# Feed-forward stage of a graph network: outputs kept in two PSUM banks, the layer norm per block on ScalarE, its scale and shift folded into the weights

## Chip, cores and metric

One NeuronCore of a Trainium2 chip runs the whole program in one launch. The metric is device time in microseconds (us); lower is better. The kernel before takes 7056.64 us (median of 3 runs, 7054.48 to 7057.89).

## What is computed

Six attention layers over a graph of 3,125 nodes (128 features each) and 100,000 edges, with normalised residual blocks around them. The change touches one stage alone, the one that stands between the first attention layer (8 heads, "gat") and the second ("tconv"). Of the reference, cut to that stage:

```python
h = elu(gat(x, ...)); h = x + h                      # x here: relu(layernorm(stream))
mu = mean(h); var = var(h)
ln = (h - mu) * rsqrt(var + 1e-05) * ln_gamma + ln_beta
inter = relu(ln @ W1 + b1)                            # 128 -> 512
stream = stream + inter @ W2 + b2 + h                 # 512 -> 128
x = relu(layernorm(stream))                           # input of the next layer
q, k, v, skip = x @ Wq + bq, x @ Wk + bk, x @ Wv + bv, x @ Wskip + bskip
```

`ln_gamma`, `ln_beta` and `b1` are not trivial here (drawn at random).

## The kernel before, in words

The program is a row of stages, each a block with its own instruction stream per engine and a barrier at its end: one that sets up the graph, and then by turns `node_stage` (work on the nodes) and `edge_sweep` (work on the edges; it gathers node rows from tables in HBM and writes partial sums to `part_tab`). The sweeps take most of the time. The changed stage is the second `node_stage`, called with `after="ffn"`.

The 25 blocks of 128 nodes (partition = node, free = feature) are worked in four chunks: blocks 0 to 3, then three chunks of 7. `chunks` holds these. Nothing is scheduled by a planner: the order on every engine is the order of the calls in the program, and engines meet at semaphores.

The stage begins by joining the sweep's partial sums (`tiles()`); then GpSimd gathers the 25 blocks' sums (`own`, L1319). Per chunk `c` there are then these pieces:

- **VectorE, `join(c)` and `use(c)`**: divide by the softmax sums (L1581 to L1585), elu with the exponential taken on ScalarE (L1636 to L1639; `elus(c)`, L1462), the moments of each row (`mean_and_spread`: L1598, L1601; the square root on ScalarE is `roots(c)`, L1457; L1606, L1607), the normalised rows into `hn` (L1642, one instruction per block), and times gamma (L1644) and plus beta (L1645) over the chunk.
- **TensorE, `feed_forward(c)`**: per block a transpose (`ffn_turn`, L1393), the product with W1 into a PSUM bank (`ffn_hidden`, L1399, 4 matmuls of 128 columns, which the profile records as 8) and the product with W2 (`ffn_out`, L1407, the same number). ScalarE stands between them: `ffn_copy` (L1467) moves the transposed block to SBUF, `ffn_relu` (L1473, 4 instructions) adds b1, clips and moves the hidden rows.
- **VectorE, `feed_forward(c)`**: the stream plus h (L1650), and plus each block's output (L1653) as it comes out of one of two banks `ffn_ps`; then `mean_and_spread` of the stream, which lets ScalarE's `inputs(c)` go.
- **The projections**: ScalarE's `inputs(c)` normalises the stream (L1492) and copies its transpose (L1507); TensorE's `multiply(c)` transposes (L1378) and multiplies (L1388, 512 columns) into one of two banks; VectorE's `products(c)` adds the bias and writes three tiles per block (L1664). SyncE stores `kv_tab` per chunk (L1291), GpSimd scatters the block's q rows to `q_tab` (L1329).

ScalarE and VectorE run these by steps, and this is what sets the order around the change. ScalarE's loop:

```python
for step in range(len(chunks) + 2):
    if step < len(chunks):
        elus(step); roots(step)
    if 1 <= step <= len(chunks):
        feed_forward(step - 1); roots(step - 1)
    if step >= 2:
        inputs(step - 2)
```

VectorE does `join(step)`, `use(step)`, `feed_forward(step - 1)`, `mean_and_spread(step - 1)` and `products(step - 2)` in each step, TensorE `feed_forward(step - 1)` and `multiply(step - 2)`.

## Time and profile before

| | us |
|---|---|
| median of 3 runs | 7056.64 |
| the profiled execution, its own time | 7060.29 |
| its span in the profile | 7058.2 |
| the stage's chunks, first `own` rows used to last product written | 1372.36 to 1510.13 |
| first instruction of the next sweep's VectorE | 1519.53 |

| engine | busy us of the span | in 1372 to 1519.5 |
|---|---|---|
| TensorE | 4367.5 | 91.36 |
| VectorE | 5261.5 | 80.79 |
| ScalarE | 3157.8 | 63.99 |
| GpSimd | 4812.4 | 45.92 |

Times in the trace count from the span's start. A row of the timeline gives an instruction or a run of like instructions with its start, its length and, in square brackets, how long its engine had been idle before it and what ended that. PE is TensorE's matmul, PEld its weight load, DVE VectorE, ACT ScalarE, POOL GpSimd. The granted clock (PEclk) is a share of TensorE's full 2.4 GHz; 0.50 is the lower level, 1.2 GHz.

### The profile page before, as it was taken

Reading aid. Unit: us, or ns where it says so; the run is one execution under the profiler, and the core shown is the slowest. Engines: PE = TensorE matmul, PEld = TensorE weight load, DVE = VectorE, ACT = ScalarE, POOL = GpSimd, SP = SyncE. Lnnn points to the kernel's source line nnn. Section 1 sums busy time; section 2 is a strip of 40 time slices with the busy share of each in tenths; the row PEclk is TensorE's granted clock in tenths of the full one; section 3 lists DMA queues with packets and bytes.
Section 4 is the critical chain, followed back from the end, with each engine's and each line's share of the span. In section 5 each row is a group of like instructions: output and inputs, shape, how many; then the busy total and the mean of one; then the engine's idle time right before and its main releaser. Section 6 shows DMA issues by size and latency. Waiting matters only on the chain. (4 is left out here: it accounts for less than half of the span.)

```text
span 7058.2 us, 100657 instructions
## 1 busy us (share of the span) xinstructions
PE 4367.5 (62%) x25901; PEld 3913.4 (55%) x25901; DVE 5261.5 (75%) x9430; ACT 3157.8 (45%) x5509; POOL 4812.4 (68%) x5080
## 2 busy tenths in 40 slices
PE   2665656467777747777755666654666664666663
PEld 1555656456666636666644555553555553555553
DVE  5766667658888848888865666655888885888887
ACT  1666666444444414444423444433555552555552
POOL 4766666347777757777757777766777774777774
PEclk6666666688898868888877777776777776777876
DMA  2777777449999949999956888864666663666663
GB/s 73 197 196 195 197 201 205 122 136 296 299 292 298 294 125 294 299 296 297 293 166 207 244 244 244 243 201 121 198 197 197 198 199 89 197 197 198 199 197 105
DMA packets 1275821, 1491.03 MB, mean 211 GB/s; under 512 B 395524, under 2 KB 967587, under 8 KB 1275252
## 3 DMA queue, kind: packets, MB, share of 16 engines
q1 hardware_dynamic: 1075428, 991.23, 44.8%
q0 software_dynamic: 199824, 493.36, 25.2%
q8 instruction: 217, 3.56, 0.2%
q14 instruction: 352, 2.88, 0.1%
HBM read 1065.64 MB, written 418.20 MB: 210 GB/s over the span
## 5 line engine op out<-in xcount | busy, mean ns | idle before, releaser
L760 POOL DMA_INDIRECT s_rows<-kv_tab,src_col x2346 | 2218.7, 946 | 733.9 <-issue 688.3
L905 PE MATMUL bank<-s_msg,s_hot 128*128 128x144 f32 (+1 forms) x9408 | 1770.3, 344 | 299.5 <-ACT s_part L800 280.9
L760 POOL DMA_INDIRECT s_rows<-xl_tab,src_col x1564 | 1476.3, 944 | 489.4 <-issue 443.5
L880 PE MATMUL bank<-s_qwin,s_hot_t 128*128 128x128 f32 (+1 forms) x9408 | 1608.7, 326 | 289.8 <-DVE s_prod L1020 156.1
L905 PEld LDWEIGHTS bank<-s_msg,s_hot 128*128 128x128 f32 x9408 | 1565.5, 239 | 352.6 <-ACT s_part L800 308.4
L880 PEld LDWEIGHTS bank<-s_qwin,s_hot_t 128*128 128x128 f32 x9408 | 1513.2, 245 | 312.0 <-issue 182.8
L800 ACT ACTIVATE s_part<-bank 128x288 f32<-128x288 f32 (+1 forms) x2352 | 914.6, 402 | 809.2 <-PE bank L905 762.8
L783 ACT ACTIVATE s_gap<-s_ranks,minus_id 128x1024 bf16<-128x1024 bf16 x588 | 673.1, 1145 | 982.4 <-DMA s_ranks<-rank_tab 980.5
L760 POOL DMA_INDIRECT s_rows<-gat_tab,src_col x782 | 739.8, 946 | 390.4 <-issue 236.3
L895 PE MATMUL bank<-ident,s_alpha 128*32 128x128 f32 (+1 forms) x588 | 185.2, 315 | 1002.3 <-DVE s_msg L1057 850.9
L794 ACT ACTIVATE s_prob<-s_diff 32x128 f32<-32x128 f32 (+1 forms) x588 | 180.5, 307 | 1233.1 <-DVE s_diff L969 1184.2
L953 DVE TENSOR_TENSOR s_hot<-bank,rank_col 128x1024 f32<-128x1024 f32 x588 | 714.7, 1215 | 0.0
L1053 DVE TENSOR_TENSOR s_msg<-s_rows,bank 128x1024 f32<-128x1024 f32 x588 | 711.6, 1210 | 0.0
L1022 DVE TENSOR_REDUCE s_alpha<-s_prod 128x16 f32<-128x512 f32 (+1 forms) x980 | 672.4, 686 | 33.6
L1020 DVE TENSOR_TENSOR s_prod<-bank,s_rows 128x512 f32<-128x512 f32 x588 | 405.6, 690 | 384.7 <-DMA s_rows<-kv_tab,src_col 357.4
L787 ACT ACTIVATE s_hot_t<-s_gap,one 128x1024 f32<-128x1024 bf16 x588 | 675.1, 1148 | 19.3
L1011 DVE TENSOR_TENSOR s_rows<-s_rows,bank 128x1024 f32<-128x1024 f32 x392 | 475.6, 1213 | 271.4 <-DMA s_rows<-kv_tab,src_col 237.6
L895 PEld LDWEIGHTS bank<-ident,s_alpha 128*32 128x32 f32 (+1 forms) x588 | 65.4, 111 | 1101.9 <-issue 1101.4
L877 PE MATMUL bank<-We,s_attr_t 128*128 128x128 f32 x3136 | 512.2, 315 | 201.7 <-DVE s_prod L1020 137.1
L877 PEld LDWEIGHTS bank<-We,s_attr_t 128*128 128x128 f32 x3136 | 445.9, 219 | 231.7 <-issue 155.5
L997 DVE TENSOR_TENSOR bank<-bank,s_rows 128x512 f32<-128x512 f32 x392 | 253.9, 692 | 166.1 <-DMA s_rows<-xl_tab,src_col 138.3
L919 PE MATMUL bank<-ident,s_attr 128*128 128x128 f32 x784 | 173.4, 363 | 300.3 <-ACT s_attr L819 291.5
(301 smaller groups left out, 4771.3 us busy)
## 6 DMA issues: line engine op xcount, KB each, us to landing
s_qwin<-q_tab SPq DMA_DIRECT2D x3920, 64.0 KB
part_tab<-s_part SPq DMA_DIRECT2D x294, 576.0 KB
part_tab<-s_part SPq DMA_DIRECT2D x294, 544.0 KB
s_ranks<-rank_tab SPq DMA_DIRECT2D x588, 256.0 KB
s_attr_t<-attr_tab SPq DMA_DIRECT2D x196, 512.0 KB
attr_tab<-s_attr_t SPq DMA_DIRECT2D x98, 512.0 KB, 5.5
s_rows<-kv_tab,src_col POOLq DMA_INDIRECT x2346
s_rows<-xl_tab,src_col POOLq DMA_INDIRECT x1564
```

The source lines that it names most:

```text
L760: pool.indirect_dma_start(out=rows[u][:, t, :], out_offset=None, in_=tab, in_offset=bass.IndirectOffsetOnAxis(ap=pl.src_col[:, i * G + t:i ...
L783: act.activation(gap[:, :], ranks[u][:, :], ACT.Abs, bias=pl.minus_id[:, 0:1]).then_inc(gap_done, 1)
L787: act.activation(hot_t[u % 2][:, :], gap[:, :], ACT.Relu, scale=-1.0, bias=pl.one[:, 0:1]).then_inc(hot_t_built, 1)
L800: act.activation(part[u][:, PAIR * c:PAIR * (c + 1), :], part_ps[c % 2][:, 0:PAIR * W].rearrange("p (t w) -> p t w", t=PAIR), ACT.Copy).th ...
L877: pe.matmul(e_ps[h][:, (t - h * per) * D:(t - h * per + 1) * D], attr_t[u][:, t * P:(t + 1) * P], w["We"][:, :], start=True, stop=True)
L880: ins = pe.matmul(q_ps[h][:, (t - h * per) * QW:(t - h * per + 1) * QW], hot_t[u % 2][:, t * P:(t + 1) * P], qwin[u][:, t, :], start=True, ...
L905: ins = pe.matmul(part_ps[c % 2][:, t * W:(t + 1) * W], hot[u][:, PAIR * c + t, :], msg[u % 2][:, PAIR * c + t, :], start=True, stop=True)
L953: v.tensor_tensor(hot[u][:, :, :], bc(iota_ps.unsqueeze(1), [P, G, P]), bc(pl.rank_col[:, bass.ds(i * G, G)].unsqueeze(2), [P, G, P]), ALU ...
L1011: v.tensor_tensor(kv, kv, bc(e.unsqueeze(2), [P, HALF, 2, D]), ALU.add).then_inc(e_used, 1)
L1020: v.tensor_tensor(prod[h][:, :, :], q, rows[u][:, t0:t1, 0:D], ALU.mult).then_inc(q_used, 1)
L1022: v.tensor_reduce(alpha[:, t0:t1, :], prod[h][:, :, :].rearrange("p t (h c) -> p t h c", c=C), AX.X, ALU.add).then_inc(alpha_done, 1)
L1053: v.tensor_tensor(out[:, :, 0:D].rearrange("p t (h c) -> p t h c", c=C), vals.rearrange("p t (h c) -> p t h c", c=C), bc(p.unsqueeze(3), [ ...
```

## The change

- A chunk's feed-forward outputs (up to 7 blocks of 128 columns) all stay in the two banks `ffn_ps`, four blocks to a bank. VectorE adds them with two instructions once the whole chunk is there. TensorE waits, ahead of a chunk's first output, until the chunk before was added.
- The normalised rows are made by ScalarE, a block at a time (`ffn_norm`), up to three blocks ahead of the block that is multiplied. Times gamma and plus beta are gone: `w1` is multiplied by gamma once, row by row, and `b1_col` gets W1ᵀ·beta, from four matmuls of one column ahead of the first chunk. Two row loads become two column loads.
- ScalarE does `feed_forward(c)` before it turns to chunk `c + 1`: `elus(c + 1)` stands behind the second block of chunk `c`, `roots(c + 1)` behind the fourth. The square roots of the stream, `roots(c - 1)`, come after chunk `c`'s first three norms; `inputs(c - 1)` follow `feed_forward(c)`.
- VectorE takes `products(c - 1)` inside `mean_and_spread(c)` of the stream, between the moments and the wait for the roots.

```diff
+            gamma_col, beta_col = sb("gamma_col", [P, 1]), sb("beta_col", [P, 1])
...
-        rows = [sb(f"row{n}", [P, D]) for n in range(len(vectors))]
+        row_vectors = vectors[2:] if after == "ffn" else vectors
+        rows = [sb(f"row{n}", [P, D]) for n in range(len(row_vectors))]
...
+                    for t, a in ((gamma_col, vectors[0]), (beta_col, vectors[1])):
+                        sp.dma_start(t[:, :], a.rearrange("(p a) -> p a", a=1), allow_slow_non_contiguous=True
+                                     ).then_inc(ffn_loaded, 16)
...
+                if after == "ffn":
+                    pe.wait_ge(ffn_loaded, 16 * 5)
+                    for k in range(PARTS):
+                        ins = pe.matmul(ps[1][:, k:k + 1], w1[:, k * P:(k + 1) * P], beta_col[:, :], start=True, stop=True)
+                    ins.then_inc(b1_folded, 1)
...
                 def ffn_turn(b):
+                    pe.wait_ge(ffn_normed, b + 1)
...
-                def ffn_out(b):
+                def ffn_out(b, slot):
                     pe.wait_ge(hidden_used, b + 1)
-                    wait(pe, ffn_added, b - 1)
+                    to = ffn_ps[slot // 4][:, (slot % 4) * D:(slot % 4 + 1) * D]
                     for k in range(PARTS):
-                        ins = pe.matmul(ffn_ps[b % 2][:, 0:D], hidden[b % 2][:, k, :], w2[:, k, :], start=(k == 0),
-                                        stop=(k == PARTS - 1))
+                        ins = pe.matmul(to, hidden[b % 2][:, k, :], w2[:, k, :], start=(k == 0), stop=(k == PARTS - 1))
                     ins.then_inc(ffn_done, 1)
...
                 def feed_forward(c):
                     if c == 0:
-                        pe.wait_ge(ffn_loaded, 48)
+                        pe.wait_ge(ffn_weights, 1)
                     lo, hi = chunks[c]
-                    pe.wait_ge(ffn_ready, c + 1)
                     ffn_turn(lo)
                     for b in range(lo, hi):
                         if b + 1 < hi:
                             ffn_turn(b + 1)
                         ffn_hidden(b)
                         if b > lo:
-                            ffn_out(b - 1)
-                    ffn_out(hi - 1)
+                            wait(pe, ffn_added, c)
+                            ffn_out(b - 1, b - 1 - lo)
+                    wait(pe, ffn_added, c)
+                    ffn_out(hi - 1, hi - 1 - lo)
...
+                def ffn_norm(b):
+                    act.activation(pl.hn[:, b, :], h[:, b, :], ACT.Identity, scale=rstd[:, b:b + 1], bias=shift[:, b:b + 1]
+                                   ).then_inc(ffn_normed, 1)
+
                 def feed_forward(c):
+                    act.wait_ge(ffn_ready, c + 1)
+                    lo, hi = chunks[c]
+                    for b in range(lo, lo + 3):
+                        ffn_norm(b)
                     if c == 0:
-                        act.wait_ge(ffn_loaded, 48)
-                    lo, hi = chunks[c]
+                        act.wait_ge(ffn_weights, 1)
+                    else:
+                        roots(c - 1)
                     ffn_copy(lo)
                     for b in range(lo, hi):
+                        if b + 3 < hi:
+                            ffn_norm(b + 3)
                         if b + 1 < hi:
                             ffn_copy(b + 1)
                         ffn_relu(b)
+                        if c + 1 < len(chunks) and b == lo + 1:
+                            elus(c + 1)
+                        if c + 1 < len(chunks) and b == lo + 3:
+                            roots(c + 1)
...
-                    for step in range(len(chunks) + 2):
-                        if step < len(chunks):
-                            elus(step)
-                            roots(step)
-                        if 1 <= step <= len(chunks):
-                            feed_forward(step - 1)
-                            roots(step - 1)
-                        if step >= 2:
-                            inputs(step - 2)
+                    elus(0)
+                    roots(0)
+                    for c in range(len(chunks)):
+                        feed_forward(c)
+                        if c >= 1:
+                            inputs(c - 1)
+                    roots(len(chunks) - 1)
+                    inputs(len(chunks) - 1)
...
-                    if proj and c >= 1 and after != "ffn":
+                    if proj and c >= 1 and x is not pl.res:
...
-                    link(mean_and_spread(c, h))
-                    for b in range(lo, hi):
-                        ins = v.tensor_scalar(pl.hn[:, b, :], h[:, b, :], rstd[:, b:b + 1], shift[:, b:b + 1], ALU.mult, ALU.add)
-                    link(ins)
-                    link(v.tensor_tensor(pl.hn[:, s, :], pl.hn[:, s, :], bc(rows[0][:, :].unsqueeze(1), [P, n, D]), ALU.mult))
-                    return v.tensor_tensor(pl.hn[:, s, :], pl.hn[:, s, :], bc(rows[1][:, :].unsqueeze(1), [P, n, D]), ALU.add)
+                    return mean_and_spread(c, h)
...
                 def feed_forward(c):
                     lo, hi = chunks[c]
                     link(v.tensor_tensor(pl.x_sb[:, lo:hi, :], pl.x_sb[:, lo:hi, :], h[:, lo:hi, :], ALU.add))
-                    for b in range(lo, hi):
-                        v.wait_ge(ffn_done, b + 1)
-                        v.tensor_tensor(pl.x_sb[:, b, :], pl.x_sb[:, b, :], ffn_ps[b % 2][:, 0:D], ALU.add).then_inc(ffn_added, 1)
-                    v.wait_ge(ffn_added, hi)
+                    v.wait_ge(ffn_done, hi)
+                    for n, b in enumerate(range(lo, hi, 4)):
+                        e = min(b + 4, hi)
+                        ins = v.tensor_tensor(pl.x_sb[:, b:e, :], pl.x_sb[:, b:e, :],
+                                              ffn_ps[n][:, 0:(e - b) * D].rearrange("p (b d) -> p b d", d=D), ALU.add)
+                    ins.then_inc(ffn_added, 1)
+                    v.wait_ge(ffn_added, c + 1)
...
+                    v.wait_ge(b1_folded, 1)
+                    link(v.tensor_tensor(b1_col[:, :], b1_col[:, :], ps[1][:, 0:PARTS], ALU.add))
+                    v.tensor_scalar(w1[:, :], w1[:, :], gamma_col[:, 0:1], None, ALU.mult).then_inc(ffn_weights, 1)
+                    for step in range(len(chunks) + 1):
                         if step < len(chunks):
                             join(step)
                             use(step).then_inc(ffn_ready, 1)
-                        if 1 <= step <= len(chunks):
+                        if step >= 1:
                             feed_forward(step - 1)
                             mean_and_spread(step - 1, pl.x_sb).then_inc(input_ready, 1)
-                        if step >= 2:
-                            products(step - 2)
+                    products(len(chunks) - 1)
```

ScalarE around the start of chunk 1's feed-forward, before (`s_below` holds the arguments and results of elu's exponential, `s_std` the roots, `s_ffn_t` the transposed block, `s_hidden` the hidden rows; L1457 128x4 is the stream of chunk 0, L1457 128x7 h of chunk 2):

```order
L1473 ACTIVATE s_hidden<-bank,s_b_col 128x128 x8
L1457 ACTIVATE s_std<-s_moments,eps 128x4
L1462 ACT_TABLE_LOAD
L1462 ACTIVATE s_below<-s_below 128x896
L1457 ACT_TABLE_LOAD
L1457 ACTIVATE s_std<-s_moments,eps 128x7
L1467 ACTIVATE s_ffn_t<-bank 128x128 x2
L1473 ACTIVATE s_hidden<-bank,s_b_col 128x128 x4
L1467 ACTIVATE s_ffn_t<-bank 128x128
L1473 ACTIVATE s_hidden<-bank,s_b_col 128x128 x4
```

The same place in the change, from the roots of chunk 1's h on (L1491 is the norm, L1480 the copy, L1486 the relu, L1475 the exponential):

```order
L1470 ACTIVATE s_std<-s_moments,eps 128x7
L1491 ACTIVATE hn<-res,s_shift,s_rstd 128x128 x3
L1470 ACTIVATE s_std<-s_moments,eps 128x4
L1480 ACTIVATE s_ffn_t<-bank 128x128
L1491 ACTIVATE hn<-res,s_shift,s_rstd 128x128
L1480 ACTIVATE s_ffn_t<-bank 128x128
L1486 ACTIVATE s_hidden<-bank,s_b_col 128x128 x4
L1491 ACTIVATE hn<-res,s_shift,s_rstd 128x128
L1480 ACTIVATE s_ffn_t<-bank 128x128
L1486 ACTIVATE s_hidden<-bank,s_b_col 128x128 x4
L1475 ACT_TABLE_LOAD
L1475 ACTIVATE s_below<-s_below 128x896
```

The exponential of chunk 2 and its table load have moved from before chunk 1's first copy to behind its second relu.

VectorE in the third step, before, from the last piece of chunk 2's `use` on (`s_q_rows` is the first write of `products(0)`, of which two more for each block follow):

```order
L1642 TENSOR_SCALAR hn<-res,s_rstd,s_shift 128x128 x7
L1644 TENSOR_TENSOR hn<-hn,s_row 128x896
L1645 TENSOR_TENSOR hn<-hn,s_row 128x896
L1650 TENSOR_TENSOR x_sb<-x_sb,res 128x896
L1653 TENSOR_TENSOR x_sb<-x_sb,bank 128x128 x7
L1598 BN_STATS s_stats<-x_sb 128x6 x7
L1601 BN_AGGR s_moments<-s_stats 128x2 x7
L1606 RECIPROCAL s_rstd<-s_std 128x7
L1607 SCALAR_TENSOR_TENSOR s_shift<-s_moments,s_rstd 128x7
L1664 TENSOR_TENSOR s_q_rows<-bank,s_bias 128x128
```

The same place in the change:

```order
L1672 TENSOR_TENSOR x_sb<-x_sb,res 128x896
L1676 TENSOR_TENSOR x_sb<-x_sb,bank 128x512
L1676 TENSOR_TENSOR x_sb<-x_sb,bank 128x384
L1625 BN_STATS s_stats<-x_sb 128x6 x7
L1628 BN_AGGR s_moments<-s_stats 128x2 x7
L1689 TENSOR_TENSOR s_q_rows<-bank,s_bias 128x128
```

The norm, gamma and beta are gone, seven adds are two, and the products of chunk 0 stand ahead of L1606 and L1607 (now L1633 and L1634), no longer behind them.

## Rows read from the trace of the kernel before

**Rows 1.** Busy time by stretch: stretch, length, PE, PEld, DVE, ACT, POOL, PEclk, DMA, GB/s.

```profile
1388.87:1399.34 10.47, 10.13 (x68) 9.92 (x68) 5.71 (x15) 5.13 (x19) 8.33 (x8) 0.77 0.24 58
...
1409.25:1425.46 16.21, 15.86 (x117) 15.48 (x117) 7.00 (x18) 9.08 (x34) 0.00 (x0) 0.85 0.00 1
1425.46:1444.30 18.84, 7.46 (x14) 3.11 (x14) 12.85 (x51) 6.86 (x15) 3.92 (x4) 0.74 0.11 42
1444.30:1460.07 15.77, 15.43 (x117) 15.04 (x117) 6.99 (x18) 8.97 (x34) 0.00 (x0) 0.88 0.01 2
1460.07:1474.09 14.02, 10.54 (x23) 4.33 (x23) 8.04 (x37) 5.13 (x17) 4.84 (x5) 0.76 0.05 19
1474.09:1488.52 14.43, 13.85 (x117) 13.28 (x117) 3.14 (x9) 8.97 (x34) 1.94 (x2) 1.00 0.22 78
1488.52:1510.13 21.61, 17.21 (x42) 6.67 (x42) 14.16 (x59) 9.29 (x29) 10.72 (x12) 0.92 0.20 74
```

**Rows 2.** Waits of TensorE from 1372 to 1519: total us, times, longest.

```profile
PE bank L1399 <- ACT s_ffn_t L1467: 25.7, 4, 9.7
PE bank L1393 <- DVE hn L1645: 23.2, 1, 23.2
PE bank L1378 <- ACT hn L1492: 9.6, 3, 3.2
```

**Rows 3.** Timeline, chunk 0 up to its first hidden product.

```profile
1372.36 0.18 DVE L1581 TENSOR_SCALAR s_share<-s_own 128x32 f32<-128x32 f32 x1 [6.32 <-DMA s_own<-part_tab,part_i]
...
1377.69 0.16 DVE L1607 SCALAR_TENSOR_TENSOR s_shift<-s_moments,s_rstd 128x4 f32<-128x4 f32 x1
...
1379.77 0.69 DVE L1645 TENSOR_TENSOR hn<-hn,s_row 128x512 f32<-128x512 f32 x1
...
1381.26 0.21 DVE L1581 TENSOR_SCALAR s_share<-s_own 128x56 f32<-128x56 f32 x1 [0.81 <-DMA s_own<-part_tab,part_i]
```

**Rows 4.** Timeline, chunk 2's join and elu ahead of chunk 1's feed-forward.

```profile
1401.65 0.20 DVE L1581 TENSOR_SCALAR s_share<-s_own 128x56 f32<-128x56 f32 x1
...
1404.46 0.95 ACT L1462 ACTIVATE s_below<-s_below 128x896 f32<-128x896 f32 x1 [1.84 <-DVE s_below L1636]
1405.43 1.28 ACT L1457 ACT_TABLE_LOAD   x1
...
1408.74 0.30 ACT L1457 ACTIVATE s_std<-s_moments,eps 128x7 f32<-128x7 f32 x1 [2.03 <-DVE s_moments L1601]
```

**Rows 5.** Timeline, one round of the block loop at full clock.

```profile
1417.53 1.15 ACT L1473 ACTIVATE s_hidden<-bank,s_b_col 128x128 f32<-128x128 f32 x4 [0.58 <-PE bank L1399]
...
1418.22 0.97 PEld L1399 LDWEIGHTS bank<-s_ffn_t,s_w 128*128 128x128 f32 x8
...
1418.54 0.29 ACT L1467 ACTIVATE s_ffn_t<-bank 128x128 f32<-128x128 f32 x1
...
1420.12 0.97 PEld L1399 LDWEIGHTS bank<-s_ffn_t,s_w 128*128 128x128 f32 x8
```

**Rows 6.** Timeline, two ScalarE norms of 128x128 with scale and shift from tiles.

```profile
1499.58 0.87 ACT L1492 ACTIVATE hn<-x_sb,s_shift,s_rstd 128x128 f32<-128x128 f32 x2
```

**Rows 7.** The page's costliest groups: a VectorE operation of 128x512 that reads PSUM.

```profile
L1020 DVE TENSOR_TENSOR s_prod<-bank,s_rows 128x512 f32<-128x512 f32 x588 | 405.6, 690 | 384.7 <-DMA s_rows<-kv_tab,src_col 357.4
```

**Rows 8.** Timeline, the moments of the stream after chunk 1.

```profile
1425.82 1.45 DVE L1598 BATCH_NORM_STATS2 s_stats<-x_sb 128x6 f32<-128x128 f32 x7
1427.31 0.58 DVE L1601 BATCH_NORM_AGGREGATE s_moments<-s_stats 128x2 f32<-128x6 f32 x7
```

**Rows 9.** Timeline, the stage's end and the next sweep's first instruction.

```profile
1512.63 0.97 POOL L1329 DMA_INDIRECT q_tab<-s_q_rows,compact_i  x1 [0.30 <-issue]
1519.53 0.29 DVE L1086 COPY bank<-iota_free 128x128 f32<-128x128 f32 x1 [9.41 <-PEq L1242]
```

**Rows 10.** Timeline, TensorE in a later sweep after two equal idle times.

```profile
1702.18 0.27 PE L895 MATMUL bank<-ident,s_alpha 128*32 128x128 f32 x1 [2.45 <-DVE s_msg L1057]
...
1711.09 0.37 PE L895 MATMUL bank<-ident,s_alpha 128*32 128x128 f32 x1 [2.45 <-DVE s_msg L1057]
```

More of the change, by code:

```diff
@@ L1191, in node_stage @@
             hidden_ps, ffn_ps = ps[4:6], ps[6:8]
-            ffn_loaded = sem("ffn_loaded")
+            assert most <= 8
+            gamma_col, beta_col = sb("gamma_col", [P, 1]), sb("beta_col", [P, 1])
+            ffn_loaded, b1_folded, ffn_weights = sem("ffn_loaded"), sem("b1_folded"), sem("ffn_weights")
+            ffn_normed = sem("ffn_normed")
             elu_args, elu_exps, ffn_ready = sem("elu_args"), sem("elu_exps"), sem("ffn_ready")
@@ L1245, in _ @@
             def _(sp):
-                for t, a in zip(rows, vectors):
+                for t, a in zip(rows, row_vectors):
                     sp.dma_start(t[:, :], a.partition_broadcast(P)).then_inc(vectors_loaded, 16)
@@ L1618, in use @@
                         if c == 0:
-                            v.wait_ge(vectors_loaded, 16 * len(vectors))
+                            v.wait_ge(vectors_loaded, 16 * len(rows))
                         r = [bc(t[:, :].unsqueeze(1), [P, n, D]) for t in rows]
@@ L1686, in _ @@
                 if after == "norm_stream":
-                    v.wait_ge(vectors_loaded, 16 * len(vectors))
+                    v.wait_ge(vectors_loaded, 16 * len(rows))
                     link(v.tensor_tensor(pl.x_sb[:, :, :], pl.x_sb[:, :, :], bc(rows[2][:, :].unsqueeze(1), [P, NB, D]), ALU.add))
@@ L1693, in _ @@
                 if after == "ffn":
-                    v.wait_ge(vectors_loaded, 16 * len(vectors))
-                    link(v.tensor_tensor(pl.x_sb[:, :, :], pl.x_sb[:, :, :], bc(rows[2][:, :].unsqueeze(1), [P, NB, D]), ALU.add))
-                    for step in range(len(chunks) + 2):
+                    v.wait_ge(vectors_loaded, 16 * len(rows))
+                    link(v.tensor_tensor(pl.x_sb[:, :, :], pl.x_sb[:, :, :], bc(rows[0][:, :].unsqueeze(1), [P, NB, D]), ALU.add))
+                    v.wait_ge(b1_folded, 1)
+                    link(v.tensor_tensor(b1_col[:, :], b1_col[:, :], ps[1][:, 0:PARTS], ALU.add))
+                    v.tensor_scalar(w1[:, :], w1[:, :], gamma_col[:, 0:1], None, ALU.mult).then_inc(ffn_weights, 1)
+                    for step in range(len(chunks) + 1):
                         if step < len(chunks):
```

## Prediction

> **What bounds the stage now.** The sweeps that fill the program are not touched, so only the stretch from 1372.36 to 1519.53 counts, 2% of the span. I cut it where TensorE passes from one chunk's piece to the next and read busy times by stretch [rows 1]. While a chunk's feed-forward runs TensorE is nearly full: 15.86 of 16.21 us, 15.43 of 15.77, 13.85 of 14.43. Between these stretches it is not: 7.46 of 18.84 us, 10.54 of 14.02, and next to nothing from 1399.34 to 1409.25. TensorE's waits name the cause [rows 2]: 25.7 us for ScalarE's copies ahead of W1's product in four chunks, 23.2 us for the first chunk's rows from VectorE, 9.6 us for the stream's norm. The copies are late by order alone. In step 2 ScalarE takes chunk 2's exponential at 1404.46, loads a table, takes the root at 1408.74, and only then turns to chunk 1, whose rows VectorE had finished in the step before [rows 4]. So what bounds the stage is VectorE's chain for the next chunk, put in series with this chunk's matmuls. The clock adds to it: stretches that open after a gap are granted 0.74 to 0.88 on average, the one without a gap before it 1.00 [rows 1].
>
> **The change, step by step.** I write the new order forward from the old durations, each instruction starting when its engine is free and its semaphore in. Every start below is an estimate from those rows.
>
> *Start of chunk 0.* Shift is done at 1377.85; L1642, gamma and beta end at 1380.46, and then the copy waits for chunk 1's exponential and root, so that the first hidden product starts at 1388.87 [rows 1, 3]. Now three norms on ScalarE follow at once. Two such take 0.87 us, 0.39 apart [rows 6], so the third is issued by 1378.8, the copy goes at 1379.3, the product at 1379.6. Gain **9.3**.
>
> *Folding gamma and beta.* Four one-column matmuls on TensorE, an add of four columns and a scaling of 128x512 on VectorE, ahead of chunk 0. The trace has none of these. From below they cost nothing: VectorE is idle for 6.32 us before the first rows land [rows 3]. From above they would be 0.69 us for the 128x512 one [rows 7] and as much again for the rest, still inside that idle time. I take nothing. If the loads were late it would be TensorE's gap before chunk 0, which is now short. Two row loads become two column loads at the same number of issues: nothing.
>
> *Chunk 0 to chunk 1.* Gathered rows of chunk 1 land at 1381.26 [rows 3]; join and clip take 2.8 us to the exponential (1401.65 to 1404.46 [rows 4]), so arguments are there at 1384.1. ScalarE reaches that place behind its second relu at 1385.1, loads a table (1.28), and the exponential (0.95) ends at 1387.4. VectorE's elu and moments take it to 1390.6, ScalarE's table load and root to 1391.5, VectorE's shift to 1392.0. VectorE then adds h, then four blocks of output (0.69 [rows 7]), and takes the stream's moments, to 1394.8; ScalarE's stream root and the copy follow; chunk 1's first hidden product starts at 1395.3. Before, 20.4 us passed between the two first products (1388.87 to 1409.25), now 15.7. Gain **4.6**.
>
> *A chunk's block loop.* At full clock a round is 1.90 us on TensorE (1418.22 to 1420.12). ScalarE's relu takes 1.01 to the next issue, with 0.58 us idle before it, and its copy fits [rows 5]. A norm of 0.39 us [rows 6] fits into the 0.58. It is paid when that cover is gone, at 1.2 GHz never (a round is 3.8 us), at full clock only behind a table load. Those are new in the loop: an exponential with its load (2.23) after the second block and a root with its load (1.6) after the fourth. TensorE has about 1.1 us of work left when ScalarE turns away, and ScalarE then needs a norm and a copy before it can go on, so each costs 1 to 1.5 us. Chunk 1 also opens at full clock if its gap is short. 14.4 us at full clock [rows 1] plus 2.1 gives 16.5 against 16.2 for chunk 1 and against 15.8 for chunk 2: loss **0.3** and **0.7**. Chunk 3 has neither, 14.4 as before: **0**.
>
> A new wait stands in TensorE's queue: output one of a chunk until VectorE has added the chunk before. VectorE does that right behind the next chunk's shift, at least 6 us before TensorE asks in chunks 2 and 3: nothing. From above, its two adds of 1.25 us.
>
> *Chunk 1 to chunk 2.* Before, 18.84 us [rows 1]: stream moments, root, products(0), then all of chunk 3's join and moments. Now ScalarE has the inputs of chunk 0 ready, so TensorE multiplies at once, fills both banks, and waits for VectorE: two adds 1.25, moments 1.45 and 0.58 and their links [rows 8], 3.4 in all. Then four blocks at about 1 us; the copy for chunk 2 waits only for the fourth. 7.0 us. Gain **11.8**. *Chunk 2 to chunk 3.* 14.02 before; now the same 3.4 and seven blocks, 10.4. Gain **3.6**.
>
> *Tail.* 21.61 before, in which products(2) began after moments and root. Now they begin before the root, but products(3) follow only after the root, norm, transpose and copy: a hole of 2.9. 21.3. Gain **0.3**. The next sweep starts 9.4 us after the last product and 6.9 after the last scatter [rows 9]. Scatters are 1.27 apart and end 1.5 us behind the products instead of 2.5, so what ends last gains 0 to 1 more.
>
> Sum: −9.3 −4.6 +0.3 −11.8 +0.7 −3.6 −0.3 = −28.6, and with half of that last point **−29**. The profiled execution is 7060.29, 3.65 above the median. 7056.64 − 29 = 7027.6, say **7028**.
>
> One unknown is the table load inside the loop. Row 1405.43 shows 1.28 us, 0.02 behind the end of the instruction before [rows 4]; I take 1.28. The Trainium skill (ScalarE: Activation LUTs, "What ACT_TABLE_LOAD costs") speaks against this change: it counts a switch of sets as about 2.66 us, with a drain of the engine ahead of the load. By that page six loads would cost an estimated 8 us more.
>
> **Rivals.**
> - *The clock falls in the new small gaps.* My order leaves eight idle times of 1.1 to 2.0 us on TensorE. In a later sweep 2.45 us idle once left the clock high (a 0.27 us matmul) and once did not (0.37) [rows 10], so it can go either way. Were the clock low after each gap, chunks would open slow as now. About 4.8 us at half speed costs 2.4 per chunk and more in the products; written forward that is 13 us: **7041**. For it: chunk 0's stretch is short and broken. Against: the one stretch that opened without a gap was granted 1.00 throughout [rows 1].
> - *The chunk at hand does not come first.* If chunk c+1's arguments come later than ScalarE reaches the exponential, ScalarE stands there and TensorE behind it. My margin is 1.0 us in chunk 0 and 1.4 in chunk 1. With 2 to 3 us lost in each of three chunks: **7036**.
> - *Loads that stop ScalarE for longer.* Inside the loop the engine has relus in flight when a load comes. If each of the six loads there cost as long again as its row (1.28 us [rows 4]), 7.7 us more: **7036**. Against: the load at 1405.43 started 0.02 behind an exponential.
> - *Slower.* The clock stays at 1.2 GHz through the stage because no stretch is unbroken. Then a round is 3.8 and a product 2.1 us, 25 blocks take 147.5 us from 1379.6, and with the tail's latency the last product is at 1529 against 1510.13: 19 us slower, **7076**. It decides once the granted clock of the stage is below about 0.65. Against: stretches of 14 us with TensorE full remain.
> - *Nothing is gained*, because the barrier or the next sweep's first loads wait for something else. Against: 9.4 us of the end are idle on every engine but GpSimd. **7057**.
>
> **Chances.** My forecast 0.66; clock in the gaps 0.13; chunk at hand 0.10; dearer loads 0.05; slower 0.02; nothing 0.04. What is more, my forward writing, laid over the old order, ended 5 us late, mostly in stretches at the lower clock, of which the change has fewer. A measurement of this kernel can tell 0.2%, 14 us, from no change: faster means below 7042.5. My forecast, the chunk-at-hand case and the dearer loads lie there (0.81), and of the clock case somewhat over half: 0.89. Within 0.2%: 0.08. Slower: 0.03. The range goes down to 7018 (the waits behind table loads not paid, the clock high throughout, 9 more) and up to 7042, which takes in the clock rival.
>
> **What would show it.** Right: TensorE's first hidden product about 1380, 9 us earlier; its waits for ScalarE's copies down from 25.7 to below 8 us; the stretch from chunk 1's last output to chunk 2's first hidden product 7 us; the next sweep's first VectorE instruction near 1491; everything behind it shifted whole. Wrong: a granted clock below 0.85 between 1395 and 1481; ScalarE waiting for `s_below` inside a chunk; L1642's work on ScalarE longer than 0.48 us each; rounds above 2 us in chunk 3, where nothing was added but the norm.

## The result, and the profile after

The change takes **7029.32 us** (median of 6 runs, 7026.59 to 7037.12), the kernel before 7057.27 on the same chip (6 runs, 7053.62 to 7066.97): a ratio of 0.996, 95% interval 0.9947 to 0.9973. It is 28 us faster, 0.4%; 7028 was predicted.

The profiled execution took 7037.12 us, its span is 7035.3. The spans differ by 22.9 us only. The first sweep, which the change does not touch, took longer in this execution: the first gathered rows are used at 1380.44, not 1372.36. In six profiles with that sweep unchanged the moment lies anywhere from 1365.1 to 1380.4, so whole spans can't be compared to within 15 us. I count from that moment, called A. From A to the next sweep's first VectorE instruction 147.17 us passed before, 119.12 now: **−28.05**. The rest of the program took 5538.7 and 5535.7.

Eight of the twelve experiments ran in two lots of four, each lot on one chip, on which every kernel took 9,678 to 9,991 us. The kernel before took 9938.13 us beside the first lot (next chunk first, products behind roots, banks by block, order alone) and 9867.58 beside the second (the change again, norm on VectorE, norm with gamma and beta on VectorE, last root early). I read them by stretches of the stage. The change ran in the second lot only, so each difference between the first lot and the change also contains whatever sets the two chips apart.

Busy time by stretch, the change, cut where TensorE passes between the pieces (length, PE, PEld, DVE, ACT, POOL, granted clock, DMA share, GB/s):

```profile
1387.48:1402.71 15.23, 11.44 (x69) 10.43 (x69) 9.85 (x34) 10.87 (x30) 11.88 (x12) 0.83 0.20 50
1402.71:1420.55 17.84, 16.14 (x119) 15.21 (x119) 8.27 (x25) 14.70 (x44) 3.84 (x4) 0.90 0.10 22
1420.55:1427.16 6.61, 4.57 (x15) 1.84 (x13) 5.87 (x27) 3.42 (x12) 1.98 (x2) 1.00 0.03 10
1427.16:1443.90 16.74, 14.71 (x119) 13.65 (x119) 8.70 (x28) 14.57 (x44) 1.94 (x2) 1.00 0.14 45
1443.90:1453.89 9.99, 7.91 (x25) 3.08 (x22) 8.33 (x36) 5.40 (x18) 4.43 (x5) 1.00 0.08 26
1453.89:1468.43 14.54, 13.79 (x119) 13.44 (x119) 1.66 (x5) 11.09 (x40) 3.20 (x3) 1.00 0.24 78
1468.43:1490.19 21.76, 17.25 (x42) 6.42 (x40) 14.73 (x60) 8.62 (x27) 11.71 (x13) 0.92 0.24 77
```

The gain is in four places. Chunk 0's first hidden product comes 9.5 us earlier and chunk 1's another 5.2 (table below). Against [rows 1] two passages are shorter: from chunk 1's last output to chunk 2's first hidden product 6.61 us instead of 18.84, and one chunk later 9.99 instead of 14.02. The blocks of chunks 1 and 2 take longer (17.84 us for 16.21, 16.74 for 15.77), those of chunk 3 and the tail hardly (14.54 for 14.43, 21.76 for 21.61). TensorE's waits in the stage, the change:

```profile
PE bank L1406 <- ACT hn L1491: 20.8, 2, 19.4
PE bank L1412 <- ACT s_ffn_t L1480: 4.9, 6, 1.9
PE bank L1400 <- DVE res L1689: 4.6, 3, 1.5
...
PE bank L1390 <- ACT hn L1520: 1.8, 1, 1.8
```

ScalarE's copies ahead of W1's product held TensorE for 25.7 us before [rows 2], now for 4.9. The long wait of 19.4 reaches back to before A, for the first rows.

| us from A | before | predicted | change |
|---|---|---|---|
| first hidden product, chunk 0 | 16.51 | 7.2 | 7.04 |
| chunk 1 | 36.9 | 22.9 | 22.3 |
| chunk 2 | 71.9 | 46.4 | 46.7 |
| chunk 3 | 101.7 | 73.4 | 73.5 |
| last product written | 137.77 | 109.2 | 109.75 |
| next sweep's first VectorE instruction | 147.17 | 118.2 | 119.12 |

### The profile page after: what moved, and what is told of

It reads as the page before. It is cut to its first block and busy times, and to the rows that moved or that the text cites. A ratio compares the mean times of both kernels' runs of the same rounds, so it can differ in the third digit from the quotient of the medians.

```text
span 7035.3 us, 100670 instructions
## 1 busy us (share of the span) xinstructions
PE 4351.4 (62%) x25909; PEld 3895.3 (55%) x25909; DVE 5245.4 (75%) x9381; ACT 3165.3 (45%) x5534; POOL 4810.8 (68%) x5080
## 5 line engine op out<-in xcount | busy, mean ns | idle before, releaser
L877 PE MATMUL bank<-We,s_attr_t 128*128 128x128 f32 x3136 | 497.2, 308 | 196.1 <-DVE s_prod L1020 133.5
```

Source lines behind the costliest of these rows:

```text
L877: pe.matmul(e_ps[h][:, (t - h * per) * D:(t - h * per + 1) * D], attr_t[u][:, t * P:(t + 1) * P], w["We"][:, :], start=True, stop=True)
```

## Experiments

My theory: the gain comes from ScalarE's order (chunk at hand first), and it can be had only because the two banks hold a chunk's outputs while VectorE is at the next chunk; the norm's place and the folding only shorten the start. The rivals are that one part alone does it, above all the shorter VectorE work (norm, gamma and beta gone), or the banks.

**The next chunk first again.** On ScalarE chunk c + 1's exponential and root stand once more ahead of chunk c's copies; all else is as in the change.

```diff
+                    if c + 1 < len(chunks):
+                        elus(c + 1)
+                        roots(c + 1)
                     ffn_copy(lo)
...
-                        if c + 1 < len(chunks) and b == lo + 1:
-                            elus(c + 1)
-                        if c + 1 < len(chunks) and b == lo + 3:
-                            roots(c + 1)
```

> The change with one part undone: ScalarE takes the next chunk's exponential and root (elus(c + 1), roots(c + 1)) ahead of this chunk's first copy, as before. Read as the stretch from the first gathered rows used to the next sweep's first VectorE instruction: 147.2 us in the kernel before, 119.1 in the change. Theory (the order on ScalarE is the gain): each of chunks 0 to 2 again waits for VectorE's join and moments, 8 to 9 us each, 24 in all: 143 us, and TensorE's waits for ScalarE's copies back above 25 us. Rival (the gain is the smaller work, gamma, beta and norm off VectorE and two adds for seven): 120 to 124 us.

The last product is written at A + 140.24; the change has 123.97 in the second lot (below). Since the start of the stage was not clean there, the kernel ran again later, with the kernel before beside it at 7064.49 us:

> The kernel of e1 (the next chunk's exponential and root ahead of this chunk's feed-forward) on another chip, since chunk 0 was disturbed there. There chunk 1's first hidden product to chunk 2's took 31 us against 24.7 in the change, and what followed was as long. Theory (order on ScalarE): chunk 0 then loses about 9 us before its first product and 6 more before chunk 1's, the stretch is 139 to 143 us, and the whole kernel 7050 us, within 10 of before. Rival (most of the difference was the disturbance): stretch below 130.

7059.22 us (10 runs, 7055.22 to 7065.34) against 7064.49 of before (19 runs): ratio 0.9991, 0.9981 to 1.0. From A to the next sweep 139.71 us: 20.6 more than the change, 7.5 less than before. TensorE's waits:

```profile
PE bank L1412 <- ACT s_ffn_t L1480: 29.8, 4, 10.9
PE bank L1406 <- ACT hn L1491: 19.3, 1, 19.3
```

With ScalarE's old order the copies' wait is back, at 29.8 us for the 25.7 of [rows 2], though the norm, the folding, the banks and VectorE's early products are those of the change. Of what is lost, 10.9 us lie ahead of chunk 0's first product (A + 17.91), 5.0 between it and chunk 1's and 6.1 between chunk 1's and chunk 2's. With all the rest in place, ScalarE's order decides over most of the gain.

**Order alone.** Here norm, gamma and beta are on VectorE as before, and the outputs go out block by block; only the orders of the change are kept (with its wait for the chunk's rows on TensorE).

> The new order alone: banks by block, norm, gamma and beta on VectorE as before; only the order of the calls is the change's. Theory: without the banks and the shorter VectorE chain the new order gives nothing, stretch 147 us as before (138 from first rows to last product). Rival (the order is the gain whatever the rest): 125 to 130 us.

A + 150.03 to the last product, which by itself says little with the start disturbed. Run again beside the last one:

> The kernel of e8 (the new order with banks by block and norm, gamma and beta on VectorE) on another chip. Theory: stretch 147 us, as before the change, and a whole time within 0.1% of before: order alone gives nothing. Rival: a part of the gain remains, stretch 130 to 140.

7062.41 us (7056.61 to 7069.19), ratio 0.9994, 0.9984 to 1.0003: no gain. From A to the next sweep 146.06 us, 1.1 less than before. Chunk 0's first product comes at A + 9.15 instead of 16.51 and chunk 1's at 32.4 instead of 36.9, but from chunk 0's to chunk 1's 23.3 us pass instead of 20.4 and from chunk 2's to chunk 3's 35.0 instead of 29.8, and that takes most of it back. Its waits name why:

```profile
PE bank L1414 <- DVE x_sb L1672: 26.2, 3, 8.9
...
PE bank L1405 <- ACT s_ffn_t L1473: 3.2, 6, 1.8
```

The copies' wait is down to 3.2 us, as in the change, and one as long (26.2) has come in its place: TensorE has filled both banks after two blocks and needs VectorE to empty one, and VectorE is at the next chunk's join, elu, moments and norm. The last of that, ahead of the longest of these waits:

```profile
1420.11 1.89 DVE L1661 TENSOR_SCALAR hn<-res,s_rstd,s_shift 128x128 f32<-128x128 f32 x7
1422.03 1.09 DVE L1663 TENSOR_TENSOR hn<-hn,s_row 128x896 f32<-128x896 f32 x1
1423.16 1.09 DVE L1664 TENSOR_TENSOR hn<-hn,s_row 128x896 f32<-128x896 f32 x1
...
1425.72 0.55 PE L1414 MATMUL bank<-s_w,s_hidden 128*128 128x128 f32 x1 [8.88 <-DVE x_sb L1672]
```

So the order alone is worth 1.1 us, and the change with only ScalarE's part of the order undone 7.5; together they are worth 28.0. The two runs don't split the change into exact halves, for VectorE's early products stand in both, but the sum of 8.6 shows that most of the gain belongs to neither by itself.

**The change again, in the second lot.**

> The change once more, a second profile. The stage from the first gathered rows to the next sweep's first VectorE instruction should be 119.1 us again, within 0.5, if the order of semaphores fixes it. The first sweep, which the change does not touch, took 8 us longer in the change's profile than in that of before: if that is a matter of the execution, it comes out otherwise here; if it is the change's doing, it stays.

9768.71 us for the whole program. The first product of chunk 0 is at A + 7.05, as in the first profile; then about 14 us are lost between A + 15 and A + 33, so the 119.1 us of the expectation became 133.2. From chunk 1's first product on, the steps (to chunk 2's, to chunk 3's, to the last product) are 24.7, 27.3 and 35.7 us, where the first profile of the change has 24.45, 26.7 and 36.3. The two other kernels that ran under both conditions agree less well: next chunk first has 30.7, 25.8 and 37.4 against 30.6, 25.8 and 36.0, order alone 33.0, 37.2 and 36.4 against 34.1, 35.0 and 35.25. So a step can be read in these lots to within about 2 us, the start can't. All that follows up to the last two runs was measured there.

**Banks by block.** The change with one block's output per bank, freed by VectorE's add of that block.

```diff
+                    wait(pe, ffn_added, b - 1)
+                    to = ffn_ps[b % 2][:, 0:D]
...
+                    for b in range(lo, hi):
+                        v.wait_ge(ffn_done, b + 1)
+                        v.tensor_tensor(pl.x_sb[:, b, :], pl.x_sb[:, b, :], ffn_ps[b % 2][:, 0:D], ALU.add).then_inc(ffn_added, 1)
```

> One part undone: outputs go to the two banks by turns, block by block, and VectorE adds each block by itself; the rest as in the change. Theory (the banks are what lets a chunk run while VectorE works on the next): TensorE stops at a chunk's third output until VectorE is through with the next chunk's moments, 4 to 6 us in each of chunks 0 to 2, and the stretch is 135 us. Rival (the banks only save VectorE instructions): 119 to 121 us.

The last product comes at A + 139.63, 15.7 us behind the change's 123.97; 4.0 of it lie in the disturbed start. The steps are 29.4, 33.7 and 36.2 us; the last, where no next chunk is joined, is as in the change, so the rest of the cost lies only where VectorE has a next chunk. The wait is named as with the order alone:

```profile
PE bank L1421 <- DVE x_sb L1674: 18.5, 3, 8.6
```

Order alone, of the same lot, differs from this kernel only in the norm, gamma and beta on VectorE, and its last product comes 10.4 us later (150.03); its first two steps are 3.5 us longer each, its last as long. Without the banks for a whole chunk that work of VectorE stands between TensorE and the bank it waits for.

**Products behind the roots.** VectorE takes the projections' products of chunk c − 1 again behind its mean and spread, and ScalarE takes the stream's root right behind the chunk's feed-forward.

```diff
                         feed_forward(c)
+                        roots(c)
                         if c >= 1:
                             inputs(c - 1)
-                    roots(len(chunks) - 1)
```

> One part undone: VectorE takes products(c - 1) behind the stream's root and shift, and ScalarE takes that root right behind feed_forward(c), ahead of inputs(c - 1), as before (the two go together, since each would wait for the other otherwise). Theory: TensorE again waits out moments, root and join between two chunks, about 5 us at each of three places beside a short tail: stretch 135 us. Rival (the products' place is worth the start of the tail alone): 122 to 123 us.

Last product at A + 142.19, 18.2 us later than the change; the steps are 28.9, 32.5 and 42.9 us, all three longer. In the last one ScalarE stood 3.28 us with no semaphore behind it, so that some 15 of the 18 us are the move's, an estimate. TensorE's wait for the stream's norm, once 1.8 us, is now

```profile
PE bank L1390 <- ACT hn L1518: 12.4, 3, 4.1
```

in each of the three passages. I had given this move little weight in the prediction, where it stands only as "multiplies at once". It is worth about as much as the banks.

**The norm on VectorE, folding kept.** `ffn_norm` is empty and VectorE writes the seven normalised blocks behind the shift.

> One part undone: the norm is made on VectorE (one instruction per block, 1.9 us for seven), gamma and beta stay folded. Theory: it lies on the path only at chunk 0 and 1, where VectorE's chain ends last; ScalarE saves as much: stretch 120 us, first hidden product of chunk 1 some 2.5 us later than in the change. Rival (ScalarE's norms fill its loop and stretch the rounds, so that VectorE would be the better place): 116 to 118 us.

Chunk 0 starts at A + 7.71 (+0.66) and the last product comes at 123.69, 0.3 before the change; chunk 1 starts 1.0 later, not 2.5. With the banks and the folding in place, which engine does the norm makes nothing that I can tell.

**Norm, gamma and beta on VectorE.** As the one before, and gamma and beta are applied to rows as in the kernel before, with no folding.

> The norm, times gamma and plus beta all on VectorE as before, nothing folded; order and banks as in the change. Theory: 4.1 us more of VectorE's chain per chunk, of which only 2 us at chunk 0, 4 at chunk 1 and little later is on the path: stretch 125 us. Rival (VectorE's chain is on the path in every chunk): 119 + 2.6 + 3 x 4.1 = 134 us.

Chunk 0 starts at A + 9.14 (+2.1), the last product comes at 126.24: +2.3. The steps are 24.0, 26.7 and 35.3 us, none longer than the change's, so what it costs lies before chunk 1; the disturbed start of both runs leaves the size open by a few microseconds, the sign and the place are plain. With a chunk's outputs in the banks, VectorE's smaller work is thus a small part of the 28 us; without them it was worth the 10.4 above.

**The last root early.** The change's only hole in the tail: with ScalarE's last root behind the fourth copy of `inputs(2)`, and VectorE's reciprocal and shift behind four of seven blocks of `products(2)`.

> A further step: the last chunk's stream root is taken by ScalarE behind the fourth copy of inputs(2), and VectorE's reciprocal and shift inside products(2), so that chunk 3's projections follow chunk 2's without a hole. Theory (the hole of 2.4 us and the slower clock behind it are on the path): last product 3 to 4 us earlier, but scatters at 1.27 us each then end last, 14 of them: stretch 116 to 117 us. Rival (scatters set the end already): 118.5 to 119 us.

Inconclusive. The last product came at A + 125.75, 1.8 later, and in the tail ScalarE and VectorE stood once each, 3.75 and 3.38 us, with no semaphore behind it, as in the lost 14 us. The last step took 38.85 us; less 3.75 it would be 35.1 against the change's 35.7, an estimate and within what these lots can tell.

**Products ahead of the stream's moments.** This goes further, and was timed beside the change on an undisturbed chip. VectorE takes `products(c - 1)` ahead of the moments of chunk c's stream; in the last chunk two blocks, then the moments, three more, the spread, and the rest. On ScalarE the stream's root comes behind the first relu instead of ahead of the first copy, and the exponential and the root of the next chunk one block later each in chunks 1 and 2 (in chunk 0 they stay). The last root comes behind the fifth copy of `inputs(2)`.

```diff
-                    else:
-                        roots(c - 1)
                     ffn_copy(lo)
...
+                        if c >= 1 and b == lo:
+                            roots(c - 1)
-                        if c + 1 < len(chunks) and b == lo + 1:
+                        if c + 1 < len(chunks) and b == lo + min(c + 1, 2):
                             elus(c + 1)
-                        if c + 1 < len(chunks) and b == lo + 3:
+                        if c + 1 < len(chunks) and b == lo + min(c + 3, 4):
                             roots(c + 1)
...
+                    if after == "ffn" and x is not pl.res and c >= 1:
+                        products(c - 1, last=chunks[c - 1][0] + 2 if c == len(chunks) - 1 else None)
                     for b in range(lo, hi):
                         ins = v.bn_stats(stats[:, b, :], x[:, b, :])
```

> A version meant to beat both. Beside the early last root of e6, VectorE does products(c - 1) ahead of the stream's moments of chunk c (in the last chunk two blocks ahead of them), so that TensorE's banks come free 2.1 us sooner between two chunks; ScalarE takes the stream's root behind the first relu, and the next chunk's exponential and root one block later. Written forward from the same durations: each of three passages 1.5 to 2.5 us shorter, the stretch from first gathered rows to the next sweep 111 to 112 us where the change takes 119.1 on an undisturbed chip. Rival (the exponential's arguments then come too late and ScalarE stands): no shorter than the change. The whole kernel would be 7 us below the change, a tenth of a per cent, less than its times can tell: 0.995 of before.

> The change again, timed beside e7 on the same chip: 0.996 of before if the chip is like the first one. On the chip of the last runs, where the whole program took 9,770 to 9,990 us, the stage lost 14 us ahead of chunk 1's first hidden product in idle times of ScalarE and TensorE that no semaphore explains; if they belong to that chip, they are absent here at 119.1 us, and the 8 us of the first sweep is seen once more.

**7018.53 us** (7015.13 to 7022.3; ratio to before 0.9947, 0.9933 to 0.996). The change beside it took 7027.88 (7024.78 to 7030.99; 0.996, 0.9946 to 0.9973). Their ranges don't touch: this version is 9.35 us faster than the change and beats both kernels. By the profiles, from A to the next sweep 109.78 us against 118.97; the latter is the change's 119.12 once more. Stretches of this version, cut at the same instructions and in the columns above:

```profile
1377.21:1390.09 12.88, 10.37 (x68) 9.18 (x69) 8.58 (x26) 10.51 (x29) 10.04 (x10) 0.90 0.22 53
1390.09:1407.50 17.41, 16.02 (x119) 15.16 (x119) 9.48 (x34) 14.87 (x45) 5.27 (x5) 0.91 0.11 26
1407.50:1412.65 5.15, 4.61 (x15) 1.76 (x13) 4.05 (x13) 3.24 (x11) 1.98 (x2) 1.00 0.05 16
...
1429.12:1437.57 8.45, 7.91 (x24) 3.09 (x21) 6.51 (x22) 5.20 (x17) 4.42 (x5) 1.00 0.09 31
...
1452.14:1470.35 18.21, 15.52 (x43) 5.88 (x40) 14.54 (x60) 8.52 (x27) 11.02 (x12) 1.00 0.28 91
```

The gain is in every passage: 5.15 us where the change has 6.61, 8.45 for 9.99, 18.21 for 21.76 in the tail, and 12.88 for 15.23 from chunk 0's first product to chunk 1's. The version moves several things at once and no run takes them apart, so which of them earns each passage is argued, not shown. In the middle passages TensorE works through the projections' two banks only as fast as VectorE empties them; now it is busy for 4.61 of 5.15 us and 7.91 of 8.45, and its wait for VectorE's writes is

```profile
PE bank L1400 <- DVE res L1701: 1.4, 1, 1.4
```

where the change has 4.6 us in three.

## Why the prediction was right

Each of its steps against the stretches of the change above (predicted, measured).

- *Start of chunk 0*: 9.3, 9.5. Three norms took 1.26 us and the product followed 1.5 us behind the first. Most of this is order too: order alone has the product at A + 9.15, 7.4 us earlier than before. The folding was hidden, as taken: its last instruction (1374.34, below) runs in VectorE's idle time ahead of the first rows, of which 5.62 us are left. The timeline of the change:

```profile
1374.34 0.49 DVE L1723 TENSOR_SCALAR s_w<-s_w,s_gamma_col 128x512 f32<-128x512 f32 x1
...
1380.44 0.18 DVE L1608 TENSOR_SCALAR s_share<-s_own 128x32 f32<-128x32 f32 x1 [5.62 <-DMA s_own<-part_tab,part_i]
...
1385.98 1.26 ACT L1491 ACTIVATE hn<-res,s_shift,s_rstd 128x128 f32<-128x128 f32 x3 [0.44 <-DVE s_shift L1634]
...
1387.48 2.08 PE L1412 MATMUL bank<-s_ffn_t,s_w 128*128 128x128 f32 x8
...
1392.68 1.28 ACT L1475 ACT_TABLE_LOAD   x1
1393.97 0.95 ACT L1475 ACTIVATE s_below<-s_below 128x896 f32<-128x896 f32 x1
1394.83 0.26 ACT L1480 ACTIVATE s_ffn_t<-bank 128x128 f32<-128x128 f32 x1
...
1400.10 0.71 PE L1406 MATMUL bank<-ident,hn 128*128 128x128 f32 x2 [1.42 <-ACT hn L1491]
...
1402.20 0.30 ACT L1470 ACTIVATE s_std<-s_moments,eps 128x4 f32<-128x4 f32 x1 [1.38 <-DVE s_moments L1628]
...
1402.71 1.87 PE L1412 MATMUL bank<-s_ffn_t,s_w 128*128 128x128 f32 x8 [1.90 <-ACT s_ffn_t L1480]
```

- *Chunk 0 to chunk 1*: 4.6, 5.2. *Chunk 1 to 2*: 11.8, 12.2. *Chunk 2 to 3*: 3.6, 4.0. *Tail*: a gain of 0.3 forecast, a loss of 0.15 measured, with a hole of 1.75 us plus its latency where 2.9 stood. The next sweep starts 9.37 us behind the last product (9.40 before); the half point I had added for the scatters did not come.
- *Chunk 2's loop*: loss 0.7, 1.0. *Chunk 3's*: 0, and 0.1. Where only the norm was added, the rounds were free within what two profiles can tell. One of chunk 3's rounds took 2.45 us, which the prediction had named as a sign of being wrong; the kernel before has one of 2.39 at the same place.
- *Chunk 1's loop*: loss 0.3, measured 1.6. This is the term that was off. I had written "Chunk 1 also opens at full clock if its gap is short". It did not: TensorE stood 1.42 us, worked 0.71, stood 1.90 again (the last rows above), and then W1's product of one block took 1.87 us, where 1.06 is the length at full clock. Cut finer (columns as above):

```profile
1400.00:1402.71 2.71, 0.66 (x3) 0.28 (x3) 2.23 (x11) 1.33 (x6) 2.10 (x3) 1.00 0.23 54
1402.71:1407.20 4.49, 4.49 (x25) 4.49 (x26) 3.77 (x7) 2.84 (x11) 3.58 (x4) 0.62 0.28 66
1407.20:1420.55 13.35, 11.65 (x96) 10.72 (x94) 4.49 (x18) 11.86 (x34) 0.26 (x1) 1.00 0.04 7
```

4.49 us at 0.62 of full clock, mostly the 1.2 GHz level, cost 4.49 × 0.38 = 1.7 us. So the rival of the clock falling in small gaps came true at one place of the loops and was worth 1.7 us there, not 13 in all: chunks 2 and 3 opened at 1.00, and so did both passages. In the tail the clock fell as well (0.92, as before the change; the prediction's 0.74 to 0.88 for stretches behind a gap had passed that stretch over).

The errors partly cancel: −9.5 −5.2 +1.6 −12.2 +1.0 −4.0 +0.1 +0.15 = −28.05, for −28.6 forecast without the half point. That the whole time came within 1.3 us of 7028 is partly luck: the first sweep alone varies by more, and the medians cover ranges of 10 to 13 us.

*The table loads.* The rows settle the unknown: the load takes 1.28 us and begins at once behind the relu before it; the exponential starts 0.01 behind the load, and its root's load at 1397.49 stands likewise between a relu and the root at 1398.79. The Trainium skill (ScalarE: Activation LUTs, "What ACT_TABLE_LOAD costs") counts a drain of the engine on top, about 2.66 us in all. The trace doesn't agree here: nothing beyond 1.28 us shows in the six loads' surroundings, and the steps' sum leaves no room for 8 us. ScalarE never stood for `s_below`: in chunk 0 VectorE had the arguments ready before ScalarE turned to them, so the rival of the late chunk did not come either, and the end moved with the last product, which puts out "nothing is gained". The granted clock was 0.91 on average from A to the last product, far from the 0.65 of the slower case.

What the prediction had wrong is its account of the causes more than its sum. It called the bound "late by order alone". The order alone, tried, gives 1.1 us: a bound that is only an order can need buffers before another order pays. The prediction gave the banks no part in the gain (they stand in it only as a wait that costs nothing and two adds of 1.25 us) and VectorE's early products hardly any; undone one by one they cost some 15 us each. It could be right in the sum all the same, because it wrote the whole change forward and never one part alone.

## What to carry to other kernels

When a wait is late by order, look at what the other engine will wait for once it is gone, and count the buffers it needs: the reorder alone was worth 1 us, the change without ScalarE's reorder 7, the whole 28. Where one engine serves two chunks, put first what empties the other's buffers (here the projections' products, with the roots that go with them: some 15 us for one move, and 9 for the next, which moved other things too), and the moments, which nobody needs yet, behind. Write the order forward instruction by instruction from old durations, and compare the result from a common moment inside the program, since untouched work ahead of it varied by 15 us.

## What the runs showed of the hardware

- **TensorE's clock after short idle times.** Three gaps of 1.5 to 1.9 us went different ways. After 1.90 us, ahead of chunk 1, the next 4.5 us were granted 0.62; there TensorE had also stood 1.42 us just before and worked only 0.71 between the two. In the passages a gap of 1.5 us, behind a chunk at full clock, left it at 1.00. In the tail, after 1.75 us, one block's product of 512 columns (recorded as two) took 1.13 us as before and the next block's 1.89; the stretch from 1481.45 to 1483.40 was granted 0.51:

```profile
1424.73 1.95 PE L1400 MATMUL bank<-s_wcat,s_ht 128*128 128x512 f32 x4 [1.52 <-DVE res L1689]
...
1479.68 0.71 PE L1390 MATMUL bank<-ident,hn 128*128 128x128 f32 x2 [1.75 <-ACT hn L1520]
1480.38 1.13 PE L1400 MATMUL bank<-s_wcat,s_ht 128*128 128x512 f32 x2
...
1481.45 1.89 PE L1400 MATMUL bank<-s_wcat,s_ht 128*128 128x512 f32 x2
```

In the tail the clock fell 1.8 us behind the end of the gap, ahead of chunk 1 it was down with the first product. In the version whose tail has no such gap the whole tail was granted 1.00.
- **Engines that stand.** In the two lots the same program took 9768.71 us where it takes 7029 otherwise. The lost time in this stage is idle time that no semaphore ends; the profile calls it "remote" or "issue" (the change in the second lot):

```profile
1621.23 2.08 PE L1412 MATMUL bank<-s_ffn_t,s_w 128*128 128x128 f32 x8 [2.28 <-issue]
...
1630.76 1.40 ACT L1486 ACTIVATE s_hidden<-bank,s_b_col 128x128 f32<-128x128 f32 x5 [9.58 <-remote]
```

What caused it was not tried. It need not be a lasting property of the chip: the first lot and the last two runs (the kernel before at 7064.49 us) have the same chip number, 5. It fell mostly between A + 10 and A + 33, and in two kernels once more in the tail (3.28 and 3.75 us of ScalarE), which made comparisons by later steps possible to within about 2 us and those of the start not.
